# LayerNorm statistics woven into the projection and down loops, a new SBUF map, merged gate and up loads and quarter-size down loads

## What is computed

```python
def ln(x):                                   # over the 2048 channels
    return (x - mean(x)) / sqrt(var(x) + 1e-5)

def attn(x):                                 # a gated linear recurrence
    xp = x @ proj_in_w.T + proj_in_b
    delta = softplus(xp @ B_w.T)             # 16 states
    h = h * sigmoid(A) + xp[:, :, None] * delta[:, None, :]   # per token
    y = h.sum(axis=1) @ C_w.T + D_param * xp
    return y @ proj_out_w.T + proj_out_b + x

def ffn(x):                                  # int8 weights, 2048 -> 8192 -> 2048
    fuse = silu((x @ w_gate) * s_gate) * ((x @ w_up) * s_up)
    return (fuse @ w_down) * s_down

x = x + ln(attn(ln(x)))
x = x + ln(ffn(ln(x)))
```

## Time and profile before

| | us |
|---|---|
| median of the two runs shown (2236.56 and 2546.12) | 2391.34 |
| the profiled execution | 2238.51 |
| its span, slowest core | 2236.9 |
| spans of the 8 cores | 2226.6 to 2236.9 |
| TensorE busy in the span | 1788.0 (80%) |
| VectorE busy | 391.2 (17%) |
| ScalarE busy | 356.4 (16%) |
| output projection, from its first matmul to its last | 438.1 to 550.9 |
| gate and up, first half | 743.6 to 1188.9 |
| down, first half | 1195.5 to 1419.6 |
| gate and up, second half | 1425.1 to 1871.0 |
| down, second half | 1876.5 to 2100.0 |
| from there to the end | 137 |

### The profile page before, as it was taken

How to read it: one execution, slowest core, us unless ns; L and a number is a source line. 1 busy time by engine, 2 the same in 40 slices (tenths; PEclk the granted TensorE clock), 3 DMA queues, 4 the chain that set the end, 5 groups by cost and what they waited for, 6 DMA issues and landing times.

```text
span 2236.9 us, 20795 instructions; the slowest of 8 cores (2226.6 to 2236.9 us)
## 1 busy us (share of the span) xinstructions
PE 1788.0 (80%) x8091; PEld 772.9 (35%) x8247; DVE 391.2 (17%) x654; ACT 356.4 (16%) x590; POOL 187.1 (8%) x358
## 2 busy tenths in 40 slices
PE   0709987499314699999998999899999998999730
PEld 0104432144000344444443444344444443444200
DVE  3170012311561311111113000011111110000055
ACT  4601210312226001100000000000000000000320
POOL 0000000000000011111110000111111110000000
PEclk9999988599656899999999999999999999999865
DMA  7003400143001244444443444344444443444104
GB/s 186 0 0 57 76 1 2 19 76 57 0 0 38 79 155 155 156 151 151 151 151 131 151 151 151 132 151 151 151 151 152 150 150 132 154 155 156 62 0 150
DMA packets 62643, 237.23 MB, mean 106 GB/s; under 512 B 8882, under 2 KB 9268, under 8 KB 54356
## 3 DMA queue, kind: packets, MB, share of 16 engines
q0 software_dynamic: 50864, 218.26, 29.9%
q1 hardware_dynamic: 11684, 17.64, 2.4%
HBM read 143.73 MB, written 8.39 MB: 68 GB/s over the span
## 4 chain that ended last, share of the span: by engine, by line
PE 76%; DVE 11%; ACT 6%; issue 3%; DMA 2%; DVEq 0%; SPq 0%; ACTq 0%; POOL 0%; POOLq 0%
PE pb L194 76%; DVE SQTT L502 1%; ACT SQTT L428 1%; DVE SCRT L710 1%; DVE SCRT L845 1%; DVE XT L713 1%; DVE XT L848 1%; ACT SCRT L644 1%; DVE YPRE L650 1%; ACT SQTT L430 1%; ACT SQTT L436 1%; DVE XN1T L505 1%; ACT DLY L208 1%; DMA WRFT<-wu_t 1%; DVE SQTT L706 1%
## 5 line engine op out<-in xcount | busy, mean ns | idle before, releaser
L194 PE MATMUL pb<-X2NAT,WRFT 128*128 128x512 bf16 x2007 | 441.8, 380 | 39.0 <-DVE X2NAT L744 35.9
L194 PE MATMUL pb<-FUSE,WRFT 128*128 128x512 bf16 x2007 | 444.7, 382 | 14.5 <-DMA WRFT<-wd_t 12.2
L194 PE MATMUL pb<-X2NBT,WRFT 128*128 128x512 bf16 x2007 | 442.7, 380 | 9.2 <-DMA WRFT<-wu_t 6.1
L194 PEld LDWEIGHTS pb<-X2NAT,WRFT 128*128 128x128 bf16 x2048 | 200.6, 98 | 281.3 <-issue 41.7
L194 PEld LDWEIGHTS pb<-FUSE,WRFT 128*128 128x128 bf16 x2048 | 201.3, 98 | 257.8 <-issue 19.6
L194 PEld LDWEIGHTS pb<-X2NBT,WRFT 128*128 128x128 bf16 x2048 | 200.7, 98 | 251.2 <-issue 11.6
L783 DVE SCALAR_TENSOR_TENSOR FUSE<-pb,SUC,SCRT 128x512 bf16<-128x512 f32 x128 | 96.1, 751 | 1011.8 <-PE pb L194 1011.8
L776 ACT ACTIVATE SCRT<-pb,SGC 128x512 f32<-128x512 f32 x128 | 87.9, 687 | 825.0 <-PE pb L194 825.0
L194 PE MATMUL pb<-SQTT,ONESB 128*1 128x512 bf16 (+1 forms) x224 | 90.1, 473 | 147.5 <-ACT SQTT L430 138.4
L194 PE MATMUL pb<-XN1T,WRIT 128*128 128x512 bf16 (+1 forms) x752 | 118.7, 318 | 36.0 <-DVE XN1T L505 35.2
L791 POOL DMA_DIRECT2D WRFT<-wg_t x124 | 65.4, 528 | 764.9 <-PE pb L194 764.9
(11 more groups left out here) (86 smaller groups left out, 662.0 us busy)
## 6 DMA issues: line engine op xcount, KB each, us to landing
WRFT<-wg_t POOLq DMA_DIRECT2D x128, 512.0 KB, 3.5
WRFT<-wu_t POOLq DMA_DIRECT2D x128, 512.0 KB, 4.2
WRFT<-wd_t POOLq DMA_DIRECT2D x64, 1024.0 KB, 4.9
WRIT<-w_in_t POOLq DMA_DIRECT2D x16, 512.0 KB, 6.3
XT<-xT SPq DMA_DIRECT2D x2, 4096.0 KB, 27.0
WROT<-w_out_t POOLq DMA_DIRECT2D x16, 512.0 KB, 5.1
out_xT<-XT SPq DMA_DIRECT2D x2, 4096.0 KB, 12.6
XT<-xT SPq DMA_DIRECT2D x1, 512.0 KB, 26.3
```

Of the source, the lines that this page charges most:

```text
L194: e.matmul(o, l, r, start=st, stop=sp))
```

## The change

- **SBUF map.** Every tile has a fixed place (`pin`). `FUSE` is one tile per half, gate and up weights have slots per half (`WGUA`, `WGUB`), down weights too (`WRDAT`, `WRDBT`); `Y2` takes the place of the normalised input of the same half. The 12 copies of `act_table` now use 128 columns. The state row is copied to bf16 directly.
- **Row sums** are kept in bf16, and the broadcast matmul is bf16 (`OODB`).
- **`emit_ln` is split**; `emit_ln_chain` does chain and apply with any two banks.
- **Output projection:** each of the 32 groups is followed by its own square on ScalarE and its two statistics matmuls on TensorE (sums in banks 4 to 7).
- **Apply of the second LayerNorm** (`outer1_apply`): each tile is followed by a copy and a square on ScalarE and two matmuls, the statistics of the third.
- **FFN:** no barriers ahead of it; the first gate group waits for its 16 input tiles one by one. Gate and up weights come in one 1 MB load. Down weights come in quarters of 512 KB in two slots of that size; for the first half the first two are issued at step 48 of gate and up. Each down group is followed by a square and two statistics matmuls; after the last group VectorE copies the rows.
- **End:** the first half's chain, apply and store are listed ahead of the second half's down loop, and the table load too; the second half's follow the loop.

```diff
+        emit_ln_chain(windows, outs, apply_fn, v_rows, SRA1, SRB1)
+
+    def emit_ln_chain(windows, outs, apply_fn, v_rows, ra=None, rb=None,
+                      ba=6, bb=7):
+        ra = SRA if ra is None else ra
+        rb = SRB if rb is None else rb
+        ood = OODB
         for wi, (c0, c1) in enumerate(windows):
...
-            mm(pb[6][:, 0:wl], OODF, SRA[0:1, c0:c1], True, True, inc=True)
+            mm(pb[ba][:, 0:wl], ood, ra[0:1, c0:c1], True, True, inc=True)
...
+            W("scalar", t_vec, vv)
+            W("scalar", t_pe, sq_prev[sl])
+            P("scalar", lambda e, t=t, l0=l0, sl=sl: e.activation(
+                out=SQT(2 + sl)[:, 0:512], in_=YATT(t, l0, l0 + 512),
+                func=AF.Square))
+            vsq = M("scalar")
+            W("tensor", t_vec, vv)
+            bsum = 6 if wi == 0 else 7
+            bsq = 4 if wi == 0 else 5
+            mm(pb[bsum][0:1, 0:512], ONESB, YATT(t, l0, l0 + 512),
+               t == 0, t == DT - 1)
+            W("tensor", t_scl, vsq)
+            sq_prev[sl] = mm(pb[bsq][0:1, 0:512], ONESB, SQT(2 + sl)[:, 0:512],
+                             t == 0, t == DT - 1)
...
-    v_yatt_all = t_vec.n
-
-    BAR()
-    WL2 = [(0, 512), (512, 1024)]
+    for b_ in (4, 5, 6, 7):
+        banks[b_].w_pe = t_pe.n
+    W("vector", t_pe, t_pe.n)
+    P("vector", lambda e: e.tensor_copy(out=SRA[0:1, 0:512], in_=pb[6][0:1, 0:512]))
+    P("vector", lambda e: e.tensor_copy(out=SRB[0:1, 0:512], in_=pb[4][0:1, 0:512]))
+    P("vector", lambda e: e.tensor_copy(out=SRA[0:1, 512:1024], in_=pb[7][0:1, 0:512]))
+    P("vector", lambda e: e.tensor_copy(out=SRB[0:1, 512:1024], in_=pb[5][0:1, 0:512]))
...
+            vxj = M("vector")
+            CB("vector")
+            W("scalar", t_vec, vxj)
+            W("scalar", t_pe, pe_j[j - 1])
+            P("scalar", lambda e, j=j, c0=c0, wl=wl: e.copy(
+                out=SQT(0)[:, 0:wl], in_=Xj(j, PAD + c0, PAD + c0 + wl)))
+            P("scalar", lambda e, j=j, c0=c0, wl=wl: e.activation(
+                out=SQT(1)[:, 0:wl], in_=Xj(j, PAD + c0, PAD + c0 + wl),
+                func=AF.Square))
+            vs2 = M("scalar")
+            W("tensor", t_scl, vs2)
+            mm(pb[4][0:1, 0:wl], ONESB, SQT(0)[:, 0:wl], j == 0, j == DT - 1)
+            pe_j[j] = mm(pb[5][0:1, 0:wl], ONESB, SQT(1)[:, 0:wl],
+                         j == 0, j == DT - 1)
+        banks[4].w_pe = banks[5].w_pe = t_pe.n
...
 
     act_table("silu_and_others")
 
-    BAR()
...
                 out=X2NW(k, j), in0=SQT(3)[:, 0:512], in1=invb[:, 0:512]))
-            CB("vector")
-        v_x2n = M("vector")
+            v_x2n_j.append(M("vector"))
+            CB("vector")
         W("gpsimd", t_pe, t_pe.n)
         for i in range(2):
-            v_wg[i] = DMA("gpsimd", s_wrf[i % 2],
-                          lambda e, i=i: e.dma_start(out=WRS(i % 2),
-                                                     in_=d_wg[i]))
-            v_wu[i] = DMA("gpsimd", s_wrf[2 + i % 2],
-                          lambda e, i=i: e.dma_start(out=WRS(2 + i % 2),
-                                                     in_=d_wu[i]))
-        W("tensor", t_vec, v_x2n)
+            v_wgu[i] = DMA("gpsimd", s_wrf[i % 2],
+                           lambda e, i=i, k=k: e.dma_start(out=WGUPW(k, i % 2),
+                                                           in_=d_wgu[i]))
...
+                if i == 0:
+                    W("tensor", t_vec, v_x2n_j[j])
+                mm(pb[bg.idx][:, 0:512],
+                   WGUPW(k, i % 2)[:, j * 128:(j + 1) * 128],
+                   X2NW(k, j), j == 0, j == DT - 1)
...
+            if i == 48 and k == 0:
+                W("gpsimd", t_pe, t_pe.n)
+                for (tt, qq) in [(0, 0), (0, 1)]:
+                    v_wd[(tt, qq)] = DMA(
+                        "gpsimd", s_wrd[qq % 2],
+                        lambda e, t=tt, q=qq, k=k: e.dma_start(
+                            out=WRDW(k, q % 2),
+                            in_=d_wd[t, q // 2, :, (q % 2) * 2048:
+                                     (q % 2 + 1) * 2048]))
+        if k == 1:
+            W("gpsimd", t_pe, t_pe.n)
+            W("gpsimd", t_vec, v_fuse_last)
+            for (tt, qq) in [(0, 0), (0, 1)]:
+                v_wd[(tt, qq)] = DMA(
+                    "gpsimd", s_wrd[qq % 2],
+                    lambda e, t=tt, q=qq, k=k: e.dma_start(
+                        out=WRDW(k, q % 2),
+                        in_=d_wd[t, q // 2, :, (q % 2) * 2048:
+                                 (q % 2 + 1) * 2048]))
         W("tensor", t_vec, v_fuse_last)
+        pe_acquire(banks[6 if k == 0 else 7])
+        pe_acquire(banks[0 if k == 0 else 1])
+        if k == 1:
+            act_table("natural_log_exp_and_others")
+            ln_state["mb_busy"] = (t_vec, v_fuse_last)
+            emit_final(0, v_fuse_last, ba=2, bb=3)
+        sqd_prev = {0: 0, 1: 0}
...
         for t in range(DT):
             bk = banks[4 + t % 2]
             pe_acquire(bk)
-            for hf in range(2):
-                W("tensor", v_wd[(t, hf)])
-                for kk in range(32):
-                    ki = hf * 32 + kk
+            for q in range(4):
+                W("tensor", v_wd[(t, q)])
+                for kk in range(16):
+                    ki = q * 16 + kk
                     mm(pb[bk.idx][:, 0:512],
-                       WRD((t * 2 + hf) % 2)[:, kk * 128:(kk + 1) * 128],
-                       FUSE(ki), ki == 0, ki == IT - 1, inc=(ki == IT - 1))
-                nt, nh = (t, hf + 1) if hf == 0 else (t + 1, 0)
-                nt2, nh2 = (nt, nh + 1) if nh == 0 else (nt + 1, 0)
-                pre = (nt2, nh2)
+                       WRDW(k, q % 2)[:, kk * 128:(kk + 1) * 128],
+                       FUSE(k, ki), ki == 0, ki == IT - 1)
+                pre = (t + (q + 2) // 4, (q + 2) % 4)
                 if pre[0] < DT and pre not in v_wd:
                     W("gpsimd", t_pe, t_pe.n)
-                    v_wd[pre] = DMA("gpsimd", s_wrd[(pre[0] * 2 + pre[1]) % 2],
-                                    lambda e, p=pre: e.dma_start(
-                                        out=WRD((p[0] * 2 + p[1]) % 2),
-                                        in_=d_wd[p[0], p[1]]))
+                    v_wd[pre] = DMA(
+                        "gpsimd", s_wrd[pre[1] % 2],
+                        lambda e, p=pre, k=k: e.dma_start(
+                            out=WRDW(k, p[1] % 2),
+                            in_=d_wd[p[0], p[1] // 2, :, (p[1] % 2) * 2048:
+                                     (p[1] % 2 + 1) * 2048]))
             bk.w_pe = t_pe.n
+            sl = t % 2
             W("scalar", t_pe, bk.w_pe)
+            W("scalar", t_pe, sqd_prev[sl])
             P("scalar", lambda e, t=t, k=k, b=bk.idx: e.activation(
                 out=Y2W(k, t), in_=pb[b][:, 0:512], func=AF.Identity,
                 scale=SDC[:, t:t + 1]))
+            CB("scalar")
+            P("scalar", lambda e, t=t, k=k, sl=sl: e.activation(
+                out=SQT(sl)[:, 0:512], in_=Y2W(k, t), func=AF.Square))
             vsc = M("scalar")
             bk.r_trk = (t_scl, vsc)
+            W("tensor", t_scl, vsc)
+            mm(pb[6 if k == 0 else 7][0:1, 0:512], ONESB, Y2W(k, t),
+               t == 0, t == DT - 1)
+            sqd_prev[sl] = mm(pb[0 if k == 0 else 1][0:1, 0:512], ONESB,
+                              SQT(sl)[:, 0:512], t == 0, t == DT - 1)
+        banks[6 if k == 0 else 7].w_pe = t_pe.n
+        banks[0 if k == 0 else 1].w_pe = t_pe.n
+        W("vector", t_pe, t_pe.n)
+        P("vector", lambda e, k=k, l0=l0: e.tensor_copy(
+            out=SRA[0:1, l0:l0 + 512], in_=pb[6 if k == 0 else 7][0:1, 0:512]))
+        P("vector", lambda e, k=k, l0=l0: e.tensor_copy(
+            out=SRB[0:1, l0:l0 + 512], in_=pb[0 if k == 0 else 1][0:1, 0:512]))
+        vrf = M("vector")
+        banks[6 if k == 0 else 7].r_trk = (t_vec, vrf)
+        banks[0 if k == 0 else 1].r_trk = (t_vec, vrf)
         v_wd = {}
+        v_rows_f[k] = t_vec.n
+        if k == 0:
+            tap("y2b", Y2AT)
+        else:
+            emit_final(1, v_rows_f[1])
     v_y2_all = t_scl.n
-
-    act_table("natural_log_exp_and_others")
-
```

More of the change, by code:

```diff
@@ L40, in __init__, with pin @@
         self.items = []
+    def pin(self, off, size, t0, t1, name):
+        size = (size + 63) & ~63
+        for (o, s, a0, a1, n) in self.items:
+            if not (a1 <= t0 or t1 <= a0) and not (o + s <= off or off + size <= o):
+                raise MemoryError(f"pin clash: {name} vs {n}")
+        self.items.append((off, size, t0, t1, name))
+        return off
     def alloc(self, size, t0, t1, name):
@@ L45, in alloc @@
                        if not (a1 <= t0 or t1 <= a0))
-        off = 0
+        holes, cur = [], 0
         for (s0, s1) in spans:
[L48 to L52, removed]
+            if s0 > cur:
+                holes.append((cur, s0))
+            cur = max(cur, s1)
+        if cur < self.cap:
```

(37 more changed lines are left out.)

392 lines of the change are left out of this document (202 added, 190 removed).

## The result

The changed kernel takes 1.0373 times as long as the one before, with a 95% interval of [1.0361, 1.0386]: about 2319.8 us beside 2236.4. The forecast was 2277.

What follows compares the result with a forecast made beforehand. About 1340 us of TensorE matmuls cannot shrink; only the seams between stages and LayerNorms move. +5.2 up to the FFN and +33.3 in FFN and tail, +38.5 on 2238.5, gave 2277 us; own range 2262 to 2295, wide range 2237 to 2350.

Steps and rivals of the forecast that it cites:

- rival (c): Clock falls in the gaps: 110 to 180 us in all 64, about 70 in half of them (2347 us); chance 0.16.
- the term: Output projection: statistics cost each of 32 groups 2.58 us that nothing covers, 82.6 us; net +57.0 us.
- Statistics under the second LayerNorm's apply: Second LayerNorm: ScalarE's about 1.2 us a tile hides in VectorE's 2.12; -36.3 us (-38 to -34).
- the store's 3: Second down stage: the first output store runs beside quarter loads with no slack, +3 us (0 to 8).
- the cost of one in-order wait per group: TensorE waits for each group's statistics: 2.58 us in 32 projection groups (82.6), 2.30 in 32 down groups (+73.6).
- the quarter loads: Down stages: the third quarter of each group is late by 0.94 us, 32 times, +30 us (0 to 81).
- the seam: Between the halves: row copies stand ahead of the second half's normalising in VectorE's order; +14.5 us, net +13.9.
- the start of the FFN: Up to the last matmul of the first gate group: without the barrier VectorE starts earlier; -13.0 us, -14.3 by stretch.
- the tail: End: the first half's chain, apply and output lie under the second down stage; -78.8 us, -76.5 by stretch.
- (a): Down stages: the quarter loads are hidden, landing at or under 2.6 us; 2247 us; chance 0.17.
- (b): Down stages: the quarter loads land as late as w_out_t's, in 5.1 us; 2328 us; chance 0.10.
- (d): TensorE runs the next group past the waiting statistics, which removes 128 us; 2149 us; chance 0.04.

Runs made afterwards that it cites:

- both fillings: The changed kernel with six, or in a second kernel three, throwaway matmuls before each projection group's wait for the add: 2300.9 us with six, 2302.2 us with three.

## Why the prediction was wrong

Most of its steps held, and the sum did not: it was short by 43.5 us, and 23.5, 8.5 and 8.2 of them lie in three stretches, where terms were missing or too small. The largest is the clock.

- **The clock in the projection: the step that failed.** The prediction had this as rival (c), with 0.16, and priced it for all 64 gaps or half of them, or none in the forecast. It came behind 11 of the projection's 32 waits: 11 x (7.87 - 6.22) = 18.2 of the 23.5 us that were missing. The other part is the warm group, 6.22 where the term had 6.04 (3.24 + 2.58 + 0.22): the group starts 0.31 and not 0.22 us after the square's matmul, and the square's matmul comes up to 0.1 later. Rows for the clock stood there, one gap of 1.84 us of the earlier trace rows that was followed by the lower level. They were read as a toss-up between two whole cases, and the forecast was built at the 2.4 GHz level; what the chip did lies between them. The wait after a projection group is of two pieces (1.5 and 0.4 us) around a lone matmul, in a cycle of 6.2 us; in the down stages one of 1.7 us comes in 17. The first lowered the clock in every third group; the second did in no group of the first down stage and, on core 3, in one of the second (8.77 us where 7.08 is usual). Why in every third one is open. That both fillings give 18 us back, with more matmuls in the stage, shows that the idle waits are the cause. The Trainium skill (TensorE: Matmul & The Clock Gate, A second HAM failure mode) describes a kernel whose short idles between groups of matmuls make the clock swing between its two levels; the trace agrees with it for the projection, 11 times in 32 groups.
- **Statistics under the second LayerNorm's apply, 8.5 us.** The prediction set ScalarE's 1.2 us a tile against VectorE's 2.12 and called it hidden. It didn't follow the buffers: the next copy into `SQT(0)` waits for the matmuls that read it, so copy, square, handoff, two matmuls at the low clock and a handoff make a ring of 2.39 us. This was a wait in the diff, `W("scalar", t_pe, pe_j[j - 1])`. With a second buffer the ring was broken, and 7.9 of the 8.5 us came back in the stretch.
- **The second down stage, 8.2 us.** From when each quarter was due, its loads were late by 21.4 us in all, 6.0 of them for the one beside the output store, where 15 and the store's 3 stood: 3.4 us. The matmuls behind that load began at the low clock (29 of them 7.83 us, beside 7.08 for 32): 1.4. The later group of 8.77 us adds 1.7, and each group's restart 0.09, 1.4 in 15 gaps. So the store's term was too small, 3 where load and clock cost 6.5 more than a usual quarter, but that is less than half of the 8.2; the four parts come to 7.9.
- **The first half's down stage, 4.6 us.** Its list has 13.2 us of waits for loads, which are 17.8 from when each quarter was due, and 15 stood: 2.8. The next group starts 0.52 us after the sum's matmul (1241.08 to 1241.60), not 0.43, 1.4 us in 15 gaps. The first matmul was held up by the last `FUSE` for 1.6 us, not 1.2.
- **Right:** the cost of one in-order wait per group (both kinds), the quarter loads (+30, and 31 came back with 1 MB loads), the seam (+14.1 beside +14.5) with its cause (13 came back), the start of the FFN (-16.3 beside -14.3), the gate and up stages, and the tail (-75.3 beside -76.5).
- **The rivals:** (a) and (b) fell with the 3.5 us at which a quarter load lands. (c) came in 12 of the 64 gaps, 11 in the projection and one in down, for 20 us where it had 70 or more. (d) fell with the waits of 1.92 and 1.71 us a group. The wide range held the time, since part of (c) was in it, and the forecast's own range, 2262 to 2295, did not; 0.48 stood on a time within 2%, and it was 3.7%.
